# Two neighbouring node tiles read one gathered block of edges

## What is computed

```python
xn = layernorm(x)
xw = einsum('nd,rdh->nrh', xn, W_rel)
agg = segment_sum(xw[src, edge_type], dst, 6250)
x = x + relu(agg + xn @ W_self + bias) + mix(xn)
x = x + ffn(layernorm(x))
```

## Time and profile before

| | us |
|---|---|
| median of three runs (lowest to highest) | 2344.6 (2341.38 to 2349.25) |
| the profiled execution | 2342.61 |
| its span, first to last instruction | 2341.0 |
| busy: TensorE matmuls, POOL, VectorE, ScalarE | 1988.8, 1713.7, 1268.4, 683.9 |

### The profile page before, as it was taken

How to read it: one execution, slowest core, us unless ns; L and a number is a source line. 1 busy time by engine, 2 the same in 40 slices (tenths; PEclk the granted TensorE clock), 3 DMA queues, 4 the chain that set the end, 5 groups by cost and what they waited for, 6 DMA issues and landing times.

```text
span 2341.0 us, 53372 instructions
## 1 busy us (share of the span) xinstructions
PE 1988.8 (85%) x18206; PEld 1629.0 (70%) x18206; DVE 1268.4 (54%) x4442; ACT 683.9 (29%) x1713; POOL 1713.7 (73%) x1789
## 2 busy tenths in 40 slices
PE   0268878879888889998898898899999898898897
PEld 0256657657666667777787787787777787787786
DVE  6766545654564555465465465455454555545543
ACT  1322222222232232333233233233233333332332
POOL 3477777777777777777777777777777777777771
PEclk9979999999999999999999999999998999999998
DMA  7555444444444444444444444444444444444441
GB/s 214 190 155 146 138 129 137 143 131 130 145 140 128 138 143 125 136 125 122 126 136 121 126 136 121 127 137 122 125 136 121 127 131 126 126 129 128 126 128 37
DMA packets 158303, 310.49 MB, mean 133 GB/s; under 512 B 37682, under 2 KB 100635, under 8 KB 157774
## 3 DMA queue, kind: packets, MB, share of 16 engines
q0 software_dynamic: 82832, 228.83, 34.4%
q1 hardware_dynamic: 73725, 78.47, 10.3%
q10 hardware_dynamic: 1508, 0.02, 0.0%
HBM read 275.24 MB, written 31.96 MB: 131 GB/s over the span
## 4 chain that ended last, share of the span: by engine, by line
PE 58%; POOL 15%; issue 9%; DVE 8%; DMA 6%; ACT 2%; DVEq 0%; POOLq 0%; ACTq 0%; SPq 0%
PE bank L1365 15%; POOL ring L537 15%; PE bank L1384 14%; PE bank L1387 7%; DMA ring<-table,idx_now 4%; PE bank L1379 4%; PE bank L1501 3%; PE bank L1480 2%; DVE hot L1011 2%; PE bank L1407 2%; PE bank L1496 1%; PE bank L1526 1%; DVE s_lo L1030 1%; PE bank L1523 1%; PE bank L1524 1%
## 5 line engine op out<-in xcount | busy, mean ns | idle before, releaser
L537 POOL DMA_INDIRECT ring<-table,idx_now x1715 | 1667.0, 972 | 515.9 <-issue 483.3
L1365 PE MATMUL bank<-hot,ring 128*128 128x256 f16 (+10 forms) x9408 | 784.7, 237 | 184.4 <-DMA ring<-table,idx_now 84.3
L1365 PEld LDWEIGHTS bank<-hot,ring 128*128 128x128 f16 x9408 | 675.7, 99 | 261.6 <-DVE hot L1011 96.6
L1011 DVE TENSOR_SCALAR hot<-iota,key_now,hot_v 128x272 f16<-128x272 f16 (+8 forms) x1723 | 514.2, 350 | 20.8 <-PE bank L1365 1.7
L1384 PE MATMUL bank<-wr,s_hi 128*128 128x256 f16 x3136 | 370.7, 278 | 0.0
L1384 PEld LDWEIGHTS bank<-wr,s_hi 128*128 128x128 f16 x3136 | 314.6, 100 | 59.3 <-issue 13.1
L685 ACT ACTIVATE s_hi<-bank 128x512 f16<-128x512 f32 x392 | 212.0, 593 | 283.1 <-PE bank L1365 280.7
L1030 DVE SCALAR_TENSOR_TENSOR s_lo<-s_hi,bank 128x512 f16<-128x512 f16 x392 | 250.4, 679 | 30.1 <-ACT s_hi L685 28.2
L1039 DVE SCALAR_TENSOR_TENSOR u_g<-bank,x_g 128x256 f32<-128x256 f32 x49 | 20.6, 421 | 315.4 <-PE bank L1387 315.4
L1387 PE MATMUL bank<-wr,s_lo 128*128 128x256 f16 x1568 | 187.2, 273 | 0.0
L1387 PEld LDWEIGHTS bank<-wr,s_lo 128*128 128x128 f16 x1568 | 153.4, 98 | 17.8
(11 more groups left out here) (228 smaller groups left out, 2021.3 us busy)
## 6 DMA issues: line engine op xcount, KB each, us to landing
ring<-table,idx_now POOLq DMA_INDIRECT x1715
work<-table SPq DMA_DIRECT2D x49, 128.0 KB
xnt_d<-work SPq DMA_DIRECT2D x49, 128.0 KB
xnt_g<-xnt_d SPq DMA_DIRECT2D x49, 128.0 KB
q2nt_d<-work SPq DMA_DIRECT2D x49, 128.0 KB
work<-q2nt_d SPq DMA_DIRECT2D x49, 128.0 KB
x_g<-x SPq DMA_DIRECT2D x48, 128.0 KB
u_d<-u_g SPq DMA_DIRECT2D x48, 128.0 KB
```

The lines of the kernel that those rows point to most:

```text
L537: pool.indirect_dma_start(ring[:, b, :], None, own, bass.IndirectOffsetOnAxis(ap=idx_now[:, parity, b:b + 1], axis=0), oob_is_err=False)\
L1011: dve.tensor_scalar(hot[:, b % OH, 0:w], iota16[:, lo * R:hi * R], key_now[:, b:b + 1], hot_v[:, b % BLOCKS:b % BLOCKS + 1], ALU.is_equal, ...
L1365: last = mm(banks[2 * (q % 2) + h][:, (l - q * BANK_N) * R:(r - q * BANK_N) * R], ring[:, b, part * D + h * P:part * D + (h + 1) * P], hot ...
```

## The change

An odd tile and the even one after it (1 and 2, 3 and 4, up to 47 and 48) share block 17. The odd tile gathers it, at places that are its own if it has an edge there that counts, and the even tile's otherwise; the even tile gathers nothing into slot 17 and multiplies what lies there by its own one-hot, whose keys are masked if the block isn't its own. Eight small operations in the prologue find pairs in which both tiles have such edges and send them down the general path; four more put the places together. Since an even tile's fourth batch has four gathers, the counts on `got[3]` go by pairs (`shared_got`), and TensorE's loop in the first stage takes two tiles a pass to know them.

```diff
+SHARED = FWD - 1
+def shared_got(pair, odd):
+    return pair * (16 * (2 * RB - 1)) + 16 * (2 * RB if odd else RB)
@@ POOL, gather
                             for r in range(TB // RB):
-                                pool.wait_ge(got[r], t * (RB * 16))
+                                if r == SHARED // RB:
+                                    pool.wait_ge(got[r], shared_got(pair, parity == 0))
+                                else:
+                                    pool.wait_ge(got[r], t * (RB * 16))
+                        if isinstance(t, int) and t == 0:
+                            pool.wait_ge(s["turned_k"], 6)
                         indices(t + 1, 1 - parity)
...
+                    if b == SHARED and parity == 0 and not (isinstance(t, int) and t == 0):
+                        continue
                     pool.indirect_dma_start(ring[:, b, :], None, own,
@@ VectorE, after bad[0:T, 3:4] (L904)
+            t1 = slice(0, T - 1)
+            two, both, other, lead = (win[t1, 2, 0:2], win[t1, 2, 2:3], win[t1, 2, 3:4], win[t1, 2, 4:5])
+            link(dve.tensor_reduce(lead, ident[t1, 1:T - 1:2], AX.X, ALU.add))
+            link(dve.tensor_tensor(two, banks[7][t1, 2:4], ec[t1, 4:6], ALU.subtract))
+            link(dve.scalar_tensor_tensor(both, two[:, 0:1], float(ROW), two[:, 1:2], ALU.mult, ALU.add))
+            link(dve.scalar_tensor_tensor(other, ident[t1, T - 2:T - 1], float(PAD_EDGES), both, ALU.mult, ALU.add))
+            link(dve.tensor_tensor(other, other, half_c[t1, 7:8], ALU.subtract))
+            link(dve.scalar_tensor_tensor(lead, other, float(2 * BWD * P + BWD * P), lead, ALU.is_gt, ALU.mult))
+            link(dve.scalar_tensor_tensor(lead, half_c[t1, 4:5], float(BWD * P), lead, ALU.is_gt, ALU.mult))
+            link(dve.tensor_tensor(bad[t1, 2:3], bad[t1, 2:3], lead, ALU.add))
@@ VectorE, after the keys are turned (L937)
+            dve.wait_ge(s["turned_s"], 5)
+            odd, even = (slice(first, first + T - 2, 2) for first in (1, 2))
+            mine, apart = gate[:, 0:T // 2], gate[:, T // 2:2 * (T // 2)]
+            link(dve.tensor_scalar(mine, key_t[:, odd, SHARED], FAR / 2, None, ALU.is_lt))
+            link(dve.tensor_tensor(apart, idx_t[:, odd, SHARED], idx_t[:, even, SHARED], ALU.subtract))
+            link(dve.tensor_tensor(apart, apart, mine, ALU.mult))
+            link(dve.tensor_tensor(idx_t[:, odd, SHARED], idx_t[:, even, SHARED], apart, ALU.add))
+            dve.nop().then_inc(s["turned_k"], 1)
@@ TensorE, prologue: a second small matmul beside spans_ready
+            mm(banks[7][0:T - 1, 2:4], ident[0:HALVES, T + 1:HALVES], ec[0:HALVES, 4:6], start=True, stop=True,
+               skip_group_check=True).then_inc(s["spans_ready"], 1)
@@ TensorE, agg
-                if b % RB == 0:
+                if b == SHARED // RB * RB:
+                    pe.wait_ge(got[b // RB], shared_got(pair, odd))
+                elif b % RB == 0:
                     pe.wait_ge(got[b // RB], (t + 1) * RB * 16)
@@ TensorE, the first stage's loop
-            with pe.Fori(2, L1 - 1) as t:
-                g_and_m(t, (MS * t - 2, MS * t - 1, MS * t))
+            with pe.Fori(1, L1 // 2) as k:
+                g_and_m(2 * k, (2 * MS * k - 2, 2 * MS * k - 1, 2 * MS * k), k, False)
+                g_and_m(2 * k + 1, (2 * MS * k + 1, 2 * MS * k + 2, 2 * MS * k + 3), k, True)
```

More of the change, by code:

```diff
@@ L523, in indices, with gather @@
                     .then_inc(s["idx_ready"], 1)
-            def gather(t, parity, own):
+            def gather(t, parity, own, pair=0):
                 pool.wait_ge(s["idx_ready"], t + 7)
@@ L545, in gather_all @@
                 with pool.Fori(0, T // 2) as k:
-                    gather(2 * k + 1, 1, own)
-                    gather(2 * k + 2, 0, own)
+                    gather(2 * k + 1, 1, own, k)
+                    gather(2 * k + 2, 0, own, k)
             pool.wait_ge(s["flag_ready"], 1)
@@ L1296, in _ @@
             pe.wait_ge(s["start_ready"], 1)
-            mm(banks[7][0:T, 0:2], ident[0:HALVES, T:HALVES], ec[0:HALVES, 4:6], start=True, stop=True)\
-                .then_inc(s["spans_ready"], 1)
+            mm(banks[7][0:T, 0:2], ident[0:HALVES, T:HALVES], ec[0:HALVES, 4:6], start=True, stop=True)
+            mm(banks[7][0:T - 1, 2:4], ident[0:HALVES, T + 1:HALVES], ec[0:HALVES, 4:6], start=True, stop=True,
+               skip_group_check=True).then_inc(s["spans_ready"], 1)
             def turn(k, source, bank):
@@ L1347, in weights_pe, with agg @@
                     pe.wait_ge(s["w16_lo"], 2)
-            def agg(t, b):
+            def agg(t, b, pair, odd):
                 lo, hi = WIN[b]
-                if b % RB == 0:
+                if b == SHARED // RB * RB:
+                    pe.wait_ge(got[b // RB], shared_got(pair, odd))
+                elif b % RB == 0:
                     pe.wait_ge(got[b // RB], (t + 1) * RB * 16)
@@ L1423, in _, with g_and_m @@
             M_AT = {0: "xt", 2: "kq", 8: "sum", 10: "qt"}
-            def g_and_m(t, ms, before=True, weights=False):
+            def g_and_m(t, ms, pair, odd, before=True, weights=False):
                 for b in range(TB):
-                    agg(t, b)
+                    agg(t, b, pair, odd)
                     if before and b == 0:
@@ L1446, in _ @@
             weights_pe(1)
-            g_and_m(0, (None, None, 0), before=False, weights=True)
-            g_and_m(1, (1, 2, 3))
-            with pe.Fori(2, L1 - 1) as t:
-                g_and_m(t, (MS * t - 2, MS * t - 1, MS * t))
-            g_and_m(L1 - 1, (T - 3, T - 2, T - 1))
+            assert L1 % 2 == 1 and T % 2 == 1
+            g_and_m(0, (None, None, 0), 0, False, before=False, weights=True)
+            g_and_m(1, (1, 2, 3), 0, True)
+            with pe.Fori(1, L1 // 2) as k:
+                g_and_m(2 * k, (2 * MS * k - 2, 2 * MS * k - 1, 2 * MS * k), k, False)
+                g_and_m(2 * k + 1, (2 * MS * k + 1, 2 * MS * k + 2, 2 * MS * k + 3), k, True)
+            g_and_m(L1 - 1, (T - 3, T - 2, T - 1), L1 // 2, False)
             pe.wait_ge(s["m_sum"], T)
@@ L1529, in _, with g_and_p @@
             STEPS = ["mix", "xt", "l1", "wt", "l2", "l3"]
-            def g_and_p(t, half, p0, at=PE_AT, before=True):
+            def g_and_p(t, half, p0, pair, odd, at=PE_AT, before=True):
                 for b in range(TB):
                     slot = half * TB + b
-                    agg(t, b)
+                    agg(t, b, pair, odd)
                     for k, a in enumerate(at[slot // PSLOT] if slot < PS * PSLOT else ()):
@@ L1539, in g_and_p @@
                         relations(t - 1)
-            g_and_p(L1, 0, 0, PE_AT_0, before=False)
-            g_and_p(L1 + 1, 1, 0, PE_AT_0)
+            g_and_p(L1, 0, 0, L1 // 2, True, PE_AT_0, before=False)
+            g_and_p(L1 + 1, 1, 0, L1 // 2 + 1, False, PE_AT_0)
             with pe.Fori(1, J2) as j:
-                g_and_p(2 * j + L1, 0, PS * j)
-                g_and_p(2 * j + (L1 + 1), 1, PS * j)
+                g_and_p(2 * j + L1, 0, PS * j, j + L1 // 2, True)
+                g_and_p(2 * j + (L1 + 1), 1, PS * j, j + (L1 // 2 + 1), False)
             p_pe(T - 1, STEPS[0])
```

## The result

| | us |
|---|---|
| kernel before, median (lowest to highest) | 2342.99 (2338.9 to 2349.25) |
| changed kernel, median (lowest to highest) | 2316.27 (2312.81 to 2319.09) |
| ratio, 95% interval | 0.9893 [0.9875, 0.9912] |
| profiled execution after: time, span | 2319.09, 2317.5 |

The change makes the kernel 1.1% faster, by 26.7 us where I had forecast 21.6. The profiled executions differ by the same order: 2341.0 - 2317.5 = 23.5 us of span. Three numbers say where these 23.5 us lie.

What follows compares the result with a forecast made beforehand. POOL's stream of 1715 gathers was taken as the bound. Gathers saved 23.1 us, checks cost 1.5, other terms nothing: 21.6 off the profiled 2342.6 gives 2321.0, plus 2.0 for the median shown, 2323.0 us; range 2315 to 2335.

Steps and rivals of the forecast that it cites:

- the general path: Whole program, rival: a pair with block 17 edges on both sides sends it there, 6 ms more; chance within 0.03.
- Twenty-four gathers at 1.26 us: POOL's stream: even tiles 2 to 48 leave out block 17's gather, 24 x 1.26 = 30.2 us less.
- How much reaches the end: Both stages: TensorE's waits for gathers decide what arrives, 10.1 + 2.5 + 9.5 + 1.0 = 23.1 us.
- POOL stays the bound to the end: Last pairs, rival: shorter loop edges prevail, all 30.2 us arrive, less 1.5: 2315.9 us; chance 0.20.
- the late tiles: Tiles 38 to 48: 7.6 us wanted, but TensorE has no gather to wait for until the last batch; 1.0 taken.
- the 9.5 us of tiles 22 to 36: Second stage, 8 even tiles: 10.1 us wanted, 9.5 us of TensorE's waits for gathers can be given back.
- Where TensorE stood in the kernel before: Last six pairs: TensorE waits for no gather; its pair and POOL's both take 88.7 us.
- POOL never waits, so POOL sets the pace: POOL between first and last gather: longest wait 0.3 us, never for a free ring place, so it sets the pace.
- The checks: Prologue, VectorE: eight more linked operations at 0.18 us lie on the path, first gather 1.5 us later.
- Folding the places: VectorE, after the keys are turned: five operations, about 0.9 us, costed at nothing; 0.9 us once without cover.
- The doubled body in the first stage: TensorE's two-tile loop, 7 passes: edge up to 6.1 us, covered by waits, costs nothing; uncovered 14 us.
- The slower rival: First stage: every code block of TensorE's doubled body stalls 4.24 us, 21 us a pair, total 2410; chance 0.05.

Runs made afterwards that it cites:

- the old edge: Changed kernel with 7 tiny 2x2 products in TensorE's prologue, moving the second stage's loop by 28 instructions: 2329.6 us, ratio 0.9962.
- the doubled loop: Kernel before with only TensorE's first-stage loop taking two tiles a round, all gathers, checks and waits as before: 2339.43 us, ratio 0.9999.

## Why the prediction was right, step by step

The forecast was 2323.0 us in a range of 2315 to 2335; 2316.3 was measured. The sign is right for the reason given: POOL (GpSimd) has 24 gathers less. The forecast gain of 21.6 us lies inside the measured interval (0.9875 to 0.9912, so 20.6 to 29.3 us), but two misses stand against each other in it: 3.0 us more lost in the prologue, some 7 more gained at the end. That they did is luck.

- **Twenty-four gathers at 1.26 us: right.** 30.2 us less 4.5 of late start are 25.7; the ratio gives 0.0107 x 2343 = 25.1 with an interval of about 4 us on either side. From first to last gather the four profiles with 1715 gathers take 2185.8 to 2192.7 us, 2188.8 in the mean, and the six with 1691 and without the old edge 2154.3 to 2167.6, 2159.1 in the mean: 29.7 less. The sharing took effect (1691 gathers) and the general path was never taken.
- **How much reaches the end: 23.1 forecast, all 30.2 came as far as the noise lets one tell, by the rival "POOL stays the bound to the end" (2315.9).** The step that failed is the one on the late tiles. I took TensorE's edge of up to 6 us as a given, and with it had 6.6 us lost in tiles 38 to 48 (1.0 of 7.6). That TensorE with such an edge is the bound was sound, but undersized: with the old edge the changed kernel is at 2329.6 us, ratio 0.9962, and has no wait for a gather left between 1064 and 2150 us, so that the 9.5 us of tiles 22 to 36 would not have come either. But the change lengthens TensorE's code ahead of the second stage's loop, and that shortened the edge from 5.0 to 2.9 us in the mean (70.3 and 40.8 over 14); the doubled loop does it alone (29.4). The body and its edge were a term of the sum, and I never asked what the change does to it.
- **Where TensorE stood in the kernel before: misread in part.** I took the missing wait for gathers in the late pairs for TensorE being the bound there. With 37 us of edges removed the kernel before took the same time. It was level with POOL, not behind it. Nor do its edges run from 5.17 to 6.1 us, as the rivals have it, but from 1.80 to 6.09.
- **"POOL never waits, so POOL sets the pace": right in the end, but not by that view.** The run with the old edge loses 13 to 16 us, and POOL's waits for TensorE show 6.4 of them, all in the last five pairs.
- **The checks: 1.5 us forecast, 4.5 measured.** Seven of them took 0.15 to 0.17 us, as the earlier trace rows told. The eighth fell into POOL's subtraction. The row that I used shows a subtraction of the line in question, and the kernel before has VectorE operations of two inputs that take 3.41 us (L876) and 4.08 us (L920) and end with a subtraction of that line or shortly behind it; I had not read them as a price.
- **Folding the places at nothing: not contradicted.** POOL's copy at block 18 shows no wait, and POOL has no idle time over 0.3 us after its first gather.
- **The doubled body in the first stage: wrong end of the bound, no harm.** I took up to 6.1 us per pass, the trace shows 0.215, and no packet on the queue of instructions between 283.1 and 838.0 us. By the figure of the Trainium skill that I had weighed against it (page "Runtime: NRT & Kernel Launch", section "Instruction fetch mechanics": 2048 instructions, blocks of 256), the doubled body of 1469 instructions fits, and the trace agrees. The second stage's body of 1641 would fit by it as well, and there the runs show both: 0.21 us in all rounds at two places of the code, in 10 and in 1 of the 14 rounds at two more, and 3.3 to 5.3 at the others.
- **The slower rival and the general path:** neither came. The rival's five blocks of code have no run of their own; the empty queue of instructions speaks against any.

What stays open: why the same code's stream from first to last gather varies by 9 us between two profiles (2167.6 and 2158.6), and by 13 over the six profiles above; single gathers of over 1.35 us from start to start make over half of it (27.4 against 22.2 us beyond 1.26 each). And by which rule a place of the loop decides between loading again, a second stall and nothing; the runs show that it does, not the rule. The sharing without the doubled loop was not tried.

## What to carry to other kernels

When work comes off the engine that sets the pace, ask how far the next engine is from setting it, and whether the edit itself moves that engine: here code added ahead of a loop was worth 16 us, by moving the loop. An engine that is hardly kept waiting is not proved to be the bound where a deep buffer lies between; read also how long the consumer still works after the producer's last piece, and how long a pair takes. And a tiny operation on a critical chain costs its neighbours' length, not its own, if it reads two tensors from SBUF while GpSimd reads there too.

## What was unexpected of the hardware

- A one-column VectorE operation with two SBUF inputs took 3.47 us in place of 0.15, because it began 0.11 us after a GpSimd subtraction of 3.57 us; in another form just the same; moved elsewhere 0.15 us again.
- The cost of the same loop on TensorE, of 1641 instructions, depends on where it lies: with 28, 52 or no more instructions ahead of it, a branch of 4.7, 0.21 or 3.9 us in the median, and idle time at 14 edges of 81.2, 17.8 and 40.8 us. At a branch of 0.21 us the queue of instructions stays empty, but for one packet in a round of the doubled loop; at a long one the body is loaded again, 8 to 10 packets of 16,384 bytes a round.
- What it is worth to shorten those edges or take them away goes by the gathers beside them: nothing with 1715, some 16 us with 1691, 49 to 55 us with 1571.
